# Cross attention: row maxima over pieces of 512 keys with the 65 left over in one, and the values copied by ScalarE with their bias folded through the output matrix

## The chip, the cores and the metric

The kernel runs on one core of a Trainium2 chip (a chip has eight; the others are idle here). The metric is the device time of one execution in microseconds (us); lower is better. One core has five engines that run their own instruction queues in order: TensorE (PE in the rows; PEld is its weight load), VectorE (DVE), ScalarE (ACT), GpSimd (POOL) and SyncE (SP, which here only issues DMAs). They wait for each other through semaphores.

## The reference, cut to what matters

The kernel computes a whole layer: self attention, cross attention on a context of 1601 tokens, a second self attention, a feed-forward block and a mixture of experts. The change lies in the cross attention alone:

```python
# x: (8, 256, 128), ctx_1024: (8, 1601, 128), H = 16 heads of 8
q = split_heads(x @ cq_w + cq_b)
k = split_heads(ctx @ ck_w + ck_b)
v = split_heads(ctx @ cv_w + cv_b)
scores = einsum('bqhd,bkhd->bhqk', q, k) / sqrt(8) + mask
probs = softmax(scores, axis=-1)
ca = einsum('bhqk,bkhd->bqhd', probs, v).reshape(8, 256, 128)
h = ca @ co_w + co_b          # then the residual and a layer norm
```

All is float32. The rows of `probs` sum to one, so a bias on `v` comes out of the attention as the same bias on every row of `ca`, and out of `h` as `cv_b @ co_w`.

## The kernel before, in words

The phases run one after another: self attention (to about 190 us), `phase_cross` (the subject here), self attention, the feed-forward block, the experts. In `phase_cross` a unit of work is a *pair* of heads of one batch: 8 batches x 8 pairs = 64 pairs, numbered g. Four engines work on it at once.

- **Maxima.** For the softmax the greatest score of every query row is found ahead of time, two pairs early. TensorE computes the scores with the queries on the partitions, in pieces that the code calls *grains* (`grain`, L1381, product L1395), and VectorE takes the maximum of each (`maxima`, L1610, L1616). The 1601 keys are cut into four pieces of 401, 401, 401 and 398 (`chunks`, L1301); with 2 heads and 2 tiles of 128 queries that is 16 grains to a pair. Four PSUM banks (`GRAIN`, L1306) hold them: a grain waits until VectorE has read the one four before it (`m_read`, L1387). After the 16th VectorE reduces the pieces to the negated maximum (`negate`, L1619, L1623), GpSimd splits it into three bf16 parts (`split_maxima`, L1708), TensorE turns it (`max_rows`, "m", L1439) and ScalarE writes it as three more rows of the queries (`place_maxima`, L1538).
- **Scores.** TensorE computes them again with the keys on the partitions (`scores`, "s", L1398, product L1413), 13 tiles to a pair of 2 x 256 columns; ScalarE takes the exponential of each (`exponentials`, L1529, L1535).
- **Values.** TensorE multiplies the exponentials with the values and a column of ones (`values`, "v", L1419, product L1433) in three *bursts* (`V_BURSTS`, L1225): tiles 0 to 3, 4 to 7 and 8 to 12. A burst waits for the exponentials of its tiles. Then ScalarE copies the result out (`read_sums`, "o", L1547, L1552).
- **Keys and values of the next batch.** In pairs 0 and 1 of a batch the next context is turned ("T", `turn_context`, L1456, taken by ScalarE, L1557), in pairs 2 and 3 its keys are made ("K", L1465, L1564), in pairs 4 and 5 its values ("V", `make_values`, L1473, product L1477). Each of T, K, V has four rounds per batch, two to a pair. The values are taken from PSUM by VectorE (`take_values`, L1649): one addition of the bias `cv_b` for each tile of 128 tokens (L1656), so four to a round and one in the last, 13 to a batch, into `VP`, where every head's 8 values are followed by a one.

The two heads of a pair lie on different rows of TensorE's array (partitions 0 to 53 and 64 to 117), so a product of one head can run beside a product of the other.

The order of the work is a list written out by `cross_plan` (L1228), which every engine walks through. In step j of 13 it puts a score tile "s" (three tiles ahead of the bursts, so tiles 0 to 2 of the next pair come in steps 10 to 12), a round of T, K or V in steps 5 and 10, the burst in steps 3, 7 and 12 (with "m" ahead of the second), and grains spread evenly: two in step 0, then one, with two in steps 3, 7 and 11, none in step 12. So 4 grains lie ahead of the first burst, 5 between the first and the second, 7 between the second and the third. Three more PSUM banks (`RING`) go round over "s", "m", "c", "e", T, K and V: each waits for the reader of the third before it (`take_bank`, L1362); "m" waits for a round of V in step 5 in this way. The last score tile of a pair is made in two halves ("h"). `grain_order` (L1254) gives each grain to the head that the last score tile did not use.

For the first batch the rounds run before the steps begin (L1521, L1696). SyncE loads the keys of a pair as soon as the scores of the pair a batch earlier are done (`load_keys`, L1791). `co_b` is added at the end of the phase by GpSimd (L1762).

Of the kernel before, what the change touches and what calls it, by code (L numbers as in the profile page):

```python
# [1222 lines left out]


V_BURSTS = (range(0, 4), range(4, 8), range(8, NTILES))  # L1225
# [26 lines left out]


def grain_order(chunks):  # L1254
# [12 lines left out]
def cross_steps(actions):  # L1267

    for step in range(-2, B * PAIRS + 1):
        b, p = divmod(step, PAIRS)  # L1270
        for what, i, ahead in cross_plan(p):
# [5 lines left out]
            elif what in "rc":  # L1277
                if 0 < b < B:
                    actions[what](b - 1, i)
            elif what == "e":  # L1280
                if b == B:
                    actions[what](b - 1, i)
            elif 0 <= step + ahead < B * PAIRS:
                actions[what](step + ahead, i)


def cross_ring():

    turns = [(what, 0, i) for what in "TKV" for i in range(4)]
    cross_steps({what: lambda unit, i, what=what: turns.append((what, unit, i)) for what in "smceTKV"})  # L1290
    return turns


def phase_cross(k):

    nc = k.nc
    T, N, G = NTILES, NCTX, 16
# [4 lines left out]
    grains = grain_order(chunks)  # L1302
    NV = len(V_BURSTS)
# [13 lines left out]
    with ExitStack() as st:  # L1317
# [13 lines left out]
        CT = k.sb("CT", [128, T * 128], stack=st)  # L1331
        KPARTS = k.sb("KPARTS", [128, 3, N], BF16, stack=st)
        KF0 = OT[:, 0:4, :].rearrange("p (c j) n -> p c (j n)", c=2)
        QF = k.CAT[:, :].rearrange("p (c n) -> p c n", c=4)
# [13 lines left out]
        k_made, k_taken, k_split, k_stored = sem("k_made"), sem("k_taken"), sem("k_split"), sem("k_stored")  # L1348
        v_made, v_taken = sem("v_made"), sem("v_taken")
        k_first, q_made, q_taken, q_stored = sem("k_first"), sem("q_made"), sem("q_taken"), sem("q_stored")  # L1350
        q_split = [sem("q_split_first"), sem("q_split_rest")]
# [8 lines left out]
        def _(pe):  # L1360

            def take_bank(what, unit, i):  # L1362

                n = turn[what, unit, i]
                if n >= 3:
# [5 lines left out]
                    elif old in "ce":  # L1371
                        pe.wait_ge(sums_done, a + 1)
                    elif old == "T":
                        pe.wait_ge(ctx_t_taken, 4 * a + j + 1)
# [6 lines left out]
            def grain(g, u):  # L1381
                n = G * g + u
                b, p = batch_of(g)
                s, qt, _, a, w = grains[u]
                half = slice(HALF * s, HALF * s + CROSS_ROWS)
                if n >= NG:
# [93 lines left out]

            prepare = {"T": turn_context, "K": make_keys, "V": make_values}
            def project_self(g):
# [38 lines left out]
            for i in range(4):  # L1521
                make_values(0, i)
            cross_steps({"s": scores, "h": last_tile, "g": grain, "v": values, "m": max_rows, "c": batch_values,
                         "e": last_values, "T": turn_context, "K": make_keys, "V": make_values})

        @block.scalar
        def _(act):
# [39 lines left out]
            def take_first_keys(i):  # L1567
# [7 lines left out]
                last.then_inc(k_taken, 1)  # L1575

            def take_normed(g):
                act.wait_ge(y_turned, g + 1)
# [19 lines left out]
            for g in range(2, 4):  # L1598
                take_normed(g)
                take_queries(g)  # L1600
            act.wait_ge(q_stored, 32 * 4)
            act.wait_ge(k_first, 6)
            act.wait_ge(k_rest, 6)
            cross_steps({"s": exponentials, "m": place_maxima, "o": read_sums, "T": take_turned, "K": take_keys})

        @block.vector
        def _(v):
            nc.vector.memset(k.PO[:, :], 0.0).then_inc(psum_cleared, 1)

            def maxima(g, u):  # L1610
                n = G * g + u
                s, qt, chunk, a, w = grains[u]
# [3 lines left out]
                nc.vector.tensor_reduce(MG[:, g % 4, 2 * s + qt, chunk:chunk + 1], GRAIN[n % NG][:, 0:w],  # L1616
                                        AX.X, ALU.max).then_inc(m_read, 1)

# [29 lines left out]

            def take_values(b, i):  # L1649
                bank = bank_of("V", b, i)  # L1650
                v.wait_ge(v_made, 4 * b + i + 1)
                if i == 0 and b >= 2:
                    v.wait_ge(pv_done, NV * PAIRS * (b - 1))
# [39 lines left out]
            normalise(3)  # L1693
            v.wait_ge(vp_set, 2)
            v.wait_ge(late_in, 48)
            for i in range(4):  # L1696
                take_values(0, i)
            cross_steps({"g": maxima, "neg": negate, "r": reciprocals, "c": scale, "e": divide_last, "V": take_values})

        @block.gpsimd  # L1700
        def _(pl):
# [891 lines left out]
```

## Time and profile before

| | us |
|---|---|
| three runs | 1243.72, 1246.9, 1254.9 (median 1246.9) |
| the profiled execution | 1246.21 |
| its span, first to last instruction | 1244.4 |
| the cross attention's steps (first maxima to last burst) | 221 to about 855 |
| busy in the whole span: PE, DVE, ACT, POOL | 1062.8, 986.2, 855.6, 407.2 |

Busy times overlap, and a product's recorded duration holds its way through the array, so that several matmuls in a row are recorded as lying over each other; the distance between starts is what one costs. The same holds, to a smaller part, for VectorE and ScalarE: a row "x7" with its whole duration is seven instructions back to back. "idle before <-X" is the time in which the engine waited ahead of the group, and who ended the wait.

### The profile page before, as it was taken

What the parts mean: (1) busy time and instruction counts of PE and PEld (TensorE: products, weight loads), DVE (VectorE), ACT (ScalarE), POOL (GpSimd) and SP (SyncE); (2) the same over time, 40 slices, a digit from 0 to 9 for tenths busy, and PEclk for the clock granted to TensorE, in tenths of its full rate; (3) what the DMA queues carried; (4) which work ended last, traced back from release to release, by engine and by line L of the source; (5) the groups of instructions that cost most, each with busy time, mean ns of one, the idle gap of its engine ahead of it and who ended that gap; (6) DMA issues with size and microseconds to landing.
All of it is one profiled execution on the core that took longest, in us unless ns stands there. A gap on an engine that the chain in (4) does not pass through costs nothing. (4 is left out here: it accounts for less than half of the span.)

```text
span 1244.4 us, 32719 instructions
## 1 busy us (share of the span) xinstructions
PE 1062.8 (85%) x11548; PEld 580.2 (47%) x11548; DVE 986.2 (79%) x2786; ACT 855.6 (69%) x1759; POOL 407.2 (33%) x838
## 2 busy tenths in 40 slices
PE   5899966899999999999999999996778879349993
PEld 2455534344444444444444444443334446338883
DVE  7688846789889898898988989992689968766664
ACT  3599944387878878788788887883379855325553
POOL 4222214050140511404105041012533425736662
PEclk8799987699999999999999999998779989669997
DMA  6943036405232143321432204100462031201113
GB/s 190 213 96 68 24 85 153 123 28 129 70 76 67 33 123 76 74 69 33 120 79 64 79 7 117 30 2 7 121 135 70 15 114 51 85 13 46 48 46 119
DMA packets 90178, 96.35 MB, mean 77 GB/s; under 512 B 18569, under 2 KB 76337, under 8 KB 90018
## 3 DMA queue, kind: packets, MB, share of 16 engines
q1 hardware_dynamic: 85922, 87.96, 28.1%
q0 software_dynamic: 2496, 5.12, 1.5%
q8 instruction: 95, 1.56, 0.5%
q10 hardware_dynamic: 1600, 1.18, 0.3%
q14 instruction: 65, 0.53, 0.2%
HBM read 67.62 MB, written 27.82 MB: 77 GB/s over the span
## 5 line engine op out<-in xcount | busy, mean ns | idle before, releaser
L1616 DVE TENSOR_REDUCE MG<-bank 128x1 f32<-128x401 f32 (+1 forms) x1024 | 515.5, 566 | 69.3 <-PE bank L1395 67.7
L1535 ACT ACTIVATE PT<-bank 128x512 f32<-128x512 f32 (+1 forms) x624 | 334.1, 598 | 53.0 <-PE bank L1413 52.7
L1413 PE MATMUL bank<-QP,KP 54*128 54x256 bf16 (+1 forms) x1664 | 253.0, 273 | 10.9 <-ACT PT L1535 1.4
L1395 PE MATMUL bank<-KP,QP 54*128 54x401 bf16 (+1 forms) x1024 | 236.0, 343 | 9.8 <-DMA KP<-ctx_k_parts 4.6
L1433 PE MATMUL bank<-PT,VP 128*9 128x256 f32 (+1 forms) x2688 | 198.0, 367 | 0.8 <-ACT XT L1535 0.8
L1706 POOL TENSOR_TENSOR MP<-MN,ZERO 128x4 bf16<-128x4 f32 x128 | 26.4, 206 | 417.6 <-DVE MN L1623 412.6
L1413 PEld LDWEIGHTS bank<-QP,KP 54*128 54x128 bf16 (+1 forms) x1664 | 111.6, 96 | 100.6 <-ACT PT L1535 24.1
L1395 PEld LDWEIGHTS bank<-KP,QP 54*128 54x128 bf16 x1024 | 75.5, 93 | 119.6 <-DVE MG L1616 98.1
L1535 ACT ACTIVATE XT<-bank 128x512 f32<-128x512 f32 (+1 forms) x208 | 117.1, 599 | 19.9 <-PE bank L1413 19.5
L1040 PE MATMUL bank<-QP,KP 51*128 51x256 bf16 x512 | 91.2, 280 | 16.4 <-DVE MN L1152 7.9
L1433 PEld LDWEIGHTS bank<-PT,VP 128*9 128x9 f32 (+1 forms) x2688 | 76.3, 90 | 58.2 <-issue 21.3
L997 PE MATMUL bank<-KP,QP 51*128 51x256 bf16 x512 | 91.6, 285 | 5.0 <-DVE MG L1146 1.6
L1146 DVE CUSTOM_DVE_ANT_0 JUNK<-bank,UQ 128x256 bf16<-128x256 f32 x256 | 91.9, 421 | 0.0
L1433 PE MATMUL bank<-XT,VP 128*9 128x256 f32 (+1 forms) x896 | 91.3, 367 | 0.0
L1152 DVE TENSOR_REDUCE MN<-bank 128x2 f32<-128x512 f32 x128 | 81.0, 682 | 3.3 <-POOL MP L1214 1.2
L1106 ACT ACTIVATE XT<-bank 128x512 f32<-128x512 f32 x128 | 73.2, 605 | 11.5 <-PE bank L1040 11.1
L1197 POOL TENSOR_TENSOR MP<-MN,ZERO 128x8 bf16<-128x8 f32 x128 | 26.4, 206 | 150.0 <-DVE MN L1159 88.6
L1040 PEld LDWEIGHTS bank<-QP,KP 51*128 51x128 bf16 x512 | 35.2, 95 | 79.1 <-issue 34.1
L959 ACT COPY QP<-bank 3x512 bf16<-3x512 bf16 x96 | 55.1, 574 | 18.1 <-PE bank L1076 16.8
L2278 PE MATMUL bank<-WUP,XP 128*128 x234 | 64.1, 409 | 2.7 <-DVE XP L2447 2.7
L1706 POOL TENSOR_TENSOR KPARTS<-XT,ZERO 128x401 bf16<-128x401 f32 (+1 forms) x56 | 47.6, 851 | 40.4 <-ACT XT L1564 38.2
L1543 ACT COPY QP<-bank 3x256 bf16<-3x256 bf16 x128 | 45.3, 354 | 19.7 <-PE bank L1444 19.0
(287 smaller groups left out, 1855.9 us busy)
## 6 DMA issues: line engine op xcount, KB each, us to landing
KP<-ctx_k_parts SPq DMA_DIRECT2D x128, 100.1 KB
ctx_k_parts<-KPARTS SPq DMA_DIRECT2D x16, 600.4 KB
KP<-ctx_k_parts SPq DMA_DIRECT2D x128, 50.0 KB
CN<-in_ctx SPq DMA_DIRECT2D x8, 768.0 KB
RAW<-in_w_gate_up SPq DMA_DIRECT2D x8, 512.0 KB, 3.8
QP<-q_parts SPq DMA_DIRECT2D x20, 192.0 KB
ctx_k_parts<-KPARTS SPq DMA_DIRECT2D x16, 200.1 KB
UQ<-bias_table SPq DMA_DIRECT2D x4, 768.0 KB, 7.2
```

The lines of the kernel that those rows point to most:

```text
L997: last = nc.tensor.matmul(bank[:, S * qt:S * (qt + 1)], k.QP[rows, p, a:a + 128], k.KP[rows, p, b * S:(b + 1) * S], start=True, stop=True)
L1040: last = nc.tensor.matmul(bank[:, S * t:S * (t + 1)], k.KP[half(s), p, a:a + 128], k.QP[half(s), p, b * S:(b + 1) * S], start=not bias, st ...
L1106: nc.scalar.activation(PT[n % 8], SCORE[n % 3][:, :], ACT.Exp).then_inc(exp_done, 1)
L1146: last = nc.vector.tensor_tensor_reduce(out=JUNK[:, 2 * (n % 2) + q, :], in0=bank[:, S * q:S * (q + 1)], in1=k.UQ[:, 2 * p + s, 128 * q:12 ...
L1152: nc.vector.tensor_reduce(MN[:, u % 3, j, s, :], bank[:, :].rearrange("p (q n) -> p q n", q=QT), AX.X, ALU.max, negate=True).then_inc(grai ...
L1395: nc.tensor.matmul(GRAIN[n % NG][:, 0:w], k.QP[half, p, b * S + 128 * qt:b * S + 128 * (qt + 1)], k.KP[half, p, a:a + w], start=True, stop ...
L1413: return nc.tensor.matmul(bank[0:rows[t], S * at:S * (at + 1)], k.KP[half, p, 128 * t:128 * t + rows[t]], k.QP[half, p, b * S:(b + 1) * S] ...
L1433: last = nc.tensor.matmul(k.PO[32 * c:32 * c + HD + 1, q:q + w], VP[b % 2][0:rows[t], t, 2 * p + s, :], PT[(T * g + n) % NP][0:rows[t], S ...
L1535: nc.scalar.activation(PT[n % NP][0:rows[t], :], bank_of("s", g, t)[0:rows[t], :], ACT.Exp).then_inc(exp_done, 1)
L1616: nc.vector.tensor_reduce(MG[:, g % 4, 2 * s + qt, chunk:chunk + 1], GRAIN[n % NG][:, 0:w], AX.X, ALU.max).then_inc(m_read, 1)
L1706: return nc.gpsimd.tensor_tensor(out, x, ZERO[:, :].broadcast_to(list(x.shape)), ALU.add)
L2278: last = nc.tensor.matmul(bank[j % 2], XP[:, j % 2, a, :], WUP[:, bass.ds(e, 1), b, n0:n0 + FF].rearrange("p a n -> p (a n)"), start=(n == ...
```

## The change

Three things change.

- **Pieces of 512.** A grain is now one of three pieces of 512 keys, or the 65 keys that are left: for each head one grain takes the 65 of both query tiles in two products of 65 columns side by side in one bank, and VectorE reduces them with one instruction of 2 x 65. A pair has 12 wide grains and 2 narrow ones, 14 instead of 16. In the plan two grains lie in step 0, one in each of steps 1 to 10, two in step 11: 4 ahead of the first burst, 4 between the first and the second, 6 between the second and the third, of which the last two are the narrow ones.
- **Values.** ScalarE copies each round (up to 128 x 512) in one instruction; VectorE's 13 additions of a batch go. In the first batch ScalarE does it ahead of its wait for the queries.
- **Bias.** Once, in the pairs 4 and 5 of the first batch, `cv_b` is turned ("R"), copied by ScalarE, multiplied with the output matrix ("W") and added to `co_b` by VectorE.

```diff
-    T, G, LEAD = NTILES, 16, 3
+    T, G, LEAD = NTILES, GRAINS, 3          # GRAINS = 4 * (NCTX // 512) + 2 = 14
...
+        if j == 3 and p in (4, 5):
+            plan.append(("RW"[p - 4], 0, 0))
...
-    rest = [[(s, qt, u, a, w) for qt in range(QT) for u, (a, w) in enumerate(chunks)] for s in range(2)]
+    rest = [[(s, qt, u) for qt in range(QT) for u in range(NCTX // WIDE)] + [(s, None, None)] for s in range(2)]
...
-                nc.tensor.matmul(GRAIN[n % NG][:, 0:w], k.QP[half, p, b * S + 128 * qt:b * S + 128 * (qt + 1)],
-                                 k.KP[half, p, a:a + w], start=True, stop=True).then_inc(m_ready, 1)
+                s, qt, chunk = grains[u]
+                if qt is not None:
+                    grain_product(g, s, qt, GRAIN[n % NG][:, :], WIDE * chunk).then_inc(m_ready, 1)
+                    return
+                for qt in range(QT):
+                    last = grain_product(g, s, qt, GRAIN[n % NG][:, REST * qt:REST * (qt + 1)], EDGE)
+                last.then_inc(m_ready, 1)
...
+            def turn_row(b, i):
+                pe.wait_ge(late_in, 48)
+                nc.tensor.transpose(take_bank("R", b, i)[:, 0:128], k.ROWS[:, ROW["cv_b"], :],
+                                    k.ID[:, :]).then_inc(row_turned, 1)
+            def project_row(b, i):
+                pe.wait_ge(row_read, 1)
+                nc.tensor.matmul(take_bank("W", b, i)[:, 0:128], BV[:, :], k.WVO[:, WQ["C"] + 1, :],
+                                 start=True, stop=True).then_inc(row_made, 1)
...
+            def take_values(b, i):                        # now on ScalarE
+                bank = bank_of("V", b, i)
+                act.wait_ge(v_made, 4 * b + i + 1)
+                if i == 0 and b >= 2:
+                    act.wait_ge(pv_done, NV * PAIRS * (b - 1))
+                m, n = rows[fours[i][-1]], len(fours[i])
+                nc.scalar.copy(VP[b % 2][0:m, 4 * i:4 * i + n, :, 0:HD],
+                               bank[0:m, 0:128 * n].rearrange("p (t h d) -> p t h d", t=n, h=H)).then_inc(v_taken, 1)
...
+                if qt is not None:
+                    out, x = MG[:, g % 4, 2 * s + qt, chunk:chunk + 1], GRAIN[n % NG][:, :]
+                else:
+                    out = MG[:, g % 4, 2 * s:2 * s + 2, N // WIDE]
+                    x = GRAIN[n % NG][:, 0:QT * REST].rearrange("p (q n) -> p q n", q=QT)
+                nc.vector.tensor_reduce(out, x, AX.X, ALU.max).then_inc(m_read, 1)
...
-            def take_values(b, i):                        # was on VectorE
-                for j, t in enumerate(fours[i]):
-                    m = rows[t]
-                    last = nc.vector.tensor_tensor(VP[b % 2][0:m, t, :, 0:HD],
-                                                   bank[0:m, 128 * j:128 * (j + 1)].rearrange("p (h d) -> p h d", h=H),
-                                                   k.ROWS[0:m, ROW["cv_b"], :].rearrange("p (h d) -> p h d", h=H),
-                                                   ALU.add)
-                last.then_inc(v_taken, 1)
+            def add_row(b, i):
+                v.wait_ge(row_made, 1)
+                row = k.ROWS[:, ROW["co_b"], :]
+                nc.vector.tensor_tensor(row, bank_of("W", b, i)[:, 0:128], row, ALU.add).then_inc(row_added, 1)
...
-            pl.wait_ge(late_in, 48)
+            pl.wait_ge(row_added, 1)
```

## Rows read from the trace of the kernel before

**Rows 1.** Windows: stretch, us, busy of PE, PEld, DVE, ACT, POOL, PEclk, DMA, GB/s

```profile
377.00:454.00 77.00, 72.89 (x870) 35.08 (x869) 67.92 (x151) 63.84 (x135) 20.34 (x47) 1.00 0.27 70
```

**Rows 2.** Costliest groups of the page: maxima (L1616, L1152), weight loads of grains (L1395)

```profile
L1616 DVE TENSOR_REDUCE MG<-bank 128x1 f32<-128x401 f32 (+1 forms) x1024 | 515.5, 566 | 69.3 <-PE bank L1395 67.7
...
L1395 PEld LDWEIGHTS bank<-KP,QP 54*128 54x128 bf16 x1024 | 75.5, 93 | 119.6 <-DVE MG L1616 98.1
...
L1152 DVE TENSOR_REDUCE MN<-bank 128x2 f32<-128x512 f32 x128 | 81.0, 682 | 3.3 <-POOL MP L1214 1.2
```

**Rows 3.** Timeline of VectorE, a pair with the reciprocals, last batch

```profile
794.14 0.17 DVE L1623 TENSOR_REDUCE MN<-MG 128x4 f32<-128x16 f32 x1
...
795.51 0.35 DVE L1632 RECIPROCAL SUMS<-SUMS 128x32 f32<-128x32 f32 x1
...
802.92 0.17 DVE L1623 TENSOR_REDUCE MN<-MG 128x4 f32<-128x16 f32 x1
```

**Rows 4.** Timeline of TensorE, a plain pair: start, duration, products

```profile
386.92 0.38 PE L1433 MATMUL bank<-XT,VP 128*9 128x256 f32 x1
387.23 0.34 PE L1395 MATMUL bank<-KP,QP 54*128 54x401 bf16 x2
387.41 0.27 PE L1413 MATMUL bank<-QP,KP 54*128 54x256 bf16 x1
...
389.07 0.40 PE L1433 MATMUL bank<-PT,VP 128*9 128x256 f32 x2
...
389.51 0.69 PE L1433 MATMUL bank<-PT,VP 128*9 128x256 f32 x8
...
392.43 0.81 PE L1433 MATMUL bank<-PT,VP 128*9 128x256 f32 x9
```

**Rows 5.** Timeline of TensorE, the pair before the last, which has no grains

```profile
840.12 0.61 PE L1433 MATMUL bank<-PT,VP 128*9 128x256 f32 x8
...
842.34 0.40 PE L1433 MATMUL bank<-PT,VP 128*9 128x256 f32 x2
...
842.43 1.03 PE L1433 MATMUL bank<-PT,VP 128*9 128x256 f32 x14
...
845.27 0.62 PE L1433 MATMUL bank<-XT,VP 128*9 128x256 f32 x8
```

**Rows 6.** Timeline of ScalarE, copies of the result, around that pair

```profile
838.42 0.37 ACT L1552 COPY OT<-bank 128x256 f32<-128x256 f32 x1 [0.51 <-PE bank L1433]
...
846.61 0.37 ACT L1552 COPY OT<-bank 128x256 f32<-128x256 f32 x1 [0.26 <-PE bank L1433]
```

**Rows 7.** Timeline of VectorE, a plain pair, the maxima after the second burst

```profile
390.51 3.46 DVE L1616 TENSOR_REDUCE MG<-bank 128x1 f32<-128x401 f32 x7 [0.41 <-PE bank L1395]
```

**Rows 8.** Timeline of TensorE, a pair with a round of V, the turning "m"

```profile
371.25 0.23 PE L1444 MATMUL bank<-IDB,MP 128*3 128x128 bf16 x2 [0.57 <-DVE VP L1656]
```

**Rows 9.** Timeline of VectorE, the same pair, the additions of that round

```profile
370.22 0.89 DVE L1656 TENSOR_TENSOR VP<-bank,LATE 128x128 f32<-128x128 f32 x4
```

**Rows 10.** Timeline of ScalarE, the same pair, exponentials around that round

```profile
370.71 1.08 ACT L1535 ACTIVATE PT<-bank 128x512 f32<-128x512 f32 x2 [0.67 <-PE bank L1413]
```

**Rows 11.** Groups of ScalarE by form, a copy into the values of self attention

```profile
L453 ACT COPY VPS<-bank 128x512 f32<-128x512 f32 x4 | 2.3, 585 | 5.5 <-PE bank L394 5.5
```

**Rows 12.** Timeline of TensorE, pair with two rounds of V, second to third burst

```profile
360.65 1.03 PE L1433 MATMUL bank<-PT,VP 128*9 128x256 f32 x14
...
362.86 1.16 PE L1477 MATMUL bank<-WVO,CT 128*128 128x128 f32 x8
...
364.78 0.62 PE L1433 MATMUL bank<-PT,VP 128*9 128x256 f32 x8
```

**Rows 13.** Timeline of TensorE, pair with two rounds of T, second to third burst

```profile
398.77 0.69 PE L1433 MATMUL bank<-XT,VP 128*9 128x256 f32 x8
...
400.64 0.66 PE L1462 MATMUL bank<-ID,CN 128*128 128x128 f32 x4
...
402.06 1.27 PE L1433 MATMUL bank<-PT,VP 128*9 128x256 f32 x24
```

More of the change, by code:

```diff
@@ L1222, in _ @@
             front.sync(sp, qk_in, (take_sums, spread_sums, give_reciprocals, place_reciprocals))
+WIDE = 512
+GRAINS = 4 * (NCTX // WIDE) + 2
 V_BURSTS = (range(0, 4), range(4, 8), range(8, NTILES))
 def cross_plan(p):
-    T, G, LEAD = NTILES, 16, 3
+    T, G, LEAD = NTILES, GRAINS, 3
     what, i = ("T", "T", "K", "K", "V", "V", None, None)[p], 2 * (p % 2)
@@ L1251, in cross_plan, with grain_order @@
     return plan + [("o", 0, 0), ("neg", 0, 2), ("split", 0, 2)]
-def grain_order(chunks):
-    rest = [[(s, qt, u, a, w) for qt in range(QT) for u, (a, w) in enumerate(chunks)] for s in range(2)]
+def grain_order():
+    rest = [[(s, qt, u) for qt in range(QT) for u in range(NCTX // WIDE)] + [(s, None, None)] for s in range(2)]
     order, half = [], 0
@@ L1282, in cross_steps @@
                     actions[what](b - 1, i)
+            elif what in "RW":
+                if b == 0:
+                    actions[what](0, i)
             elif 0 <= step + ahead < B * PAIRS:
@@ L1289, in cross_ring @@
     turns = [(what, 0, i) for what in "TKV" for i in range(4)]
-    cross_steps({what: lambda unit, i, what=what: turns.append((what, unit, i)) for what in "smceTKV"})
+    cross_steps({what: lambda unit, i, what=what: turns.append((what, unit, i)) for what in "smceTKVRW"})
     return turns
@@ L1296, in phase_cross @@
     nc = k.nc
-    T, N, G = NTILES, NCTX, 16
+    T, N, G = NTILES, NCTX, GRAINS
     rows = [min(128, N - 128 * t) for t in range(T)]
@@ L1301, in phase_cross @@
     chunks = [(c * CW, min(CW, N - c * CW)) for c in range(4)]
-    grains = grain_order(chunks)
+    grains = grain_order()
+    EDGE = WIDE * (N // WIDE)
+    REST = N - EDGE
     NV = len(V_BURSTS)
@@ L1332, in phase_cross @@
         KPARTS = k.sb("KPARTS", [128, 3, N], BF16, stack=st)
+        BV = k.sb("BV", [128, 128], stack=st)
         KF0 = OT[:, 0:4, :].rearrange("p (c j) n -> p c (j n)", c=2)
@@ L1349, in phase_cross @@
         v_made, v_taken = sem("v_made"), sem("v_taken")
+        row_turned, row_read, row_made, row_added = (sem(n) for n in ("row_turned", "row_read", "row_made", "row_added"))
         k_first, q_made, q_taken, q_stored = sem("k_first"), sem("q_made"), sem("q_taken"), sem("q_stored")
@@ L1372, in take_bank @@
                         pe.wait_ge(sums_done, a + 1)
+                    elif old == "R":
+                        pe.wait_ge(row_read, 1)
+                    elif old == "W":
+                        pe.wait_ge(row_added, 1)
                     elif old == "T":
@@ L1383, in grain @@
                 b, p = batch_of(g)
-                s, qt, _, a, w = grains[u]
-                half = slice(HALF * s, HALF * s + CROSS_ROWS)
                 if n >= NG:
@@ L1394, in grain, with grain_product @@
                     pe.wait_ge(kp_in[p], LOADS * (b + 1))
-                nc.tensor.matmul(GRAIN[n % NG][:, 0:w], k.QP[half, p, b * S + 128 * qt:b * S + 128 * (qt + 1)],
-                                 k.KP[half, p, a:a + w], start=True, stop=True).then_inc(m_ready, 1)
+                s, qt, chunk = grains[u]
[5 more added lines that the diff above has]
+                last.then_inc(m_ready, 1)
+            def grain_product(g, s, qt, out, a):
+                b, p = batch_of(g)
+                half = slice(HALF * s, HALF * s + CROSS_ROWS)
+                return nc.tensor.matmul(out, k.QP[half, p, b * S + 128 * qt:b * S + 128 * (qt + 1)],
+                                        k.KP[half, p, a:a + out.shape[1]], start=True, stop=True)
             def scores(g, i):
@@ L1479, in make_values @@
                 last.then_inc(v_made, 1)
[L1481 removed]
+            def turn_row(b, i):
[3 more added lines that the diff above has]
+            def project_row(b, i):
+                pe.wait_ge(row_read, 1)
+                nc.tensor.matmul(take_bank("W", b, i)[:, 0:128], BV[:, :], k.WVO[:, WQ["C"] + 1, :],
+                                 start=True, stop=True).then_inc(row_made, 1)
             def project_self(g):
@@ L1523, in _ @@
             cross_steps({"s": scores, "h": last_tile, "g": grain, "v": values, "m": max_rows, "c": batch_values,
-                         "e": last_values, "T": turn_context, "K": make_keys, "V": make_values})
+                         "e": last_values, "T": turn_context, "K": make_keys, "V": make_values, "R": turn_row,
+                         "W": project_row})
         @block.scalar
@@ L1575, in take_first_keys, with read_row @@
                 last.then_inc(k_taken, 1)
+            def take_values(b, i):
[6 more added lines that the diff above has]
+                               bank[0:m, 0:128 * n].rearrange("p (t h d) -> p t h d", t=n, h=H)).then_inc(v_taken, 1)
+            def read_row(b, i):
+                act.wait_ge(row_turned, 1)
+                nc.scalar.copy(BV[:, :], bank_of("R", b, i)[:, 0:128]).then_inc(row_read, 1)
             def take_normed(g):
@@ L1600, in _ @@
                 take_queries(g)
+            act.wait_ge(vp_set, 2)
+            for i in range(4):
+                take_values(0, i)
             act.wait_ge(q_stored, 32 * 4)
@@ L1603, in _ @@
             act.wait_ge(k_rest, 6)
-            cross_steps({"s": exponentials, "m": place_maxima, "o": read_sums, "T": take_turned, "K": take_keys})
+            cross_steps({"s": exponentials, "m": place_maxima, "o": read_sums, "T": take_turned, "K": take_keys,
+                         "V": take_values, "R": read_row})
         @block.vector
@@ L1611, in maxima @@
                 n = G * g + u
-                s, qt, chunk, a, w = grains[u]
                 if u == 0 and g >= 4:
@@ L1615, in maxima @@
                 v.wait_ge(m_ready, n + 1)
-                nc.vector.tensor_reduce(MG[:, g % 4, 2 * s + qt, chunk:chunk + 1], GRAIN[n % NG][:, 0:w],
-                                        AX.X, ALU.max).then_inc(m_read, 1)
+                s, qt, chunk = grains[u]
+                if qt is not None:
[4 more added lines that the diff above has]
+                nc.vector.tensor_reduce(out, x, AX.X, ALU.max).then_inc(m_read, 1)
             def negate(g, i):
@@ L1693, in _ @@
             normalise(3)
-            v.wait_ge(vp_set, 2)
             v.wait_ge(late_in, 48)
-            for i in range(4):
-                take_values(0, i)
-            cross_steps({"g": maxima, "neg": negate, "r": reciprocals, "c": scale, "e": divide_last, "V": take_values})
+            cross_steps({"g": maxima, "neg": negate, "r": reciprocals, "c": scale, "e": divide_last, "W": add_row})
         @block.gpsimd
```

4 lines of the change are left out of this document (removed).

## The prediction

> **What bounds the kernel now.** I read the page first, then the windows over the cross attention, then the timelines of single pairs, engine by engine. In a stretch of about eight pairs three engines look full: of 77 us PE is busy for 72.9, DVE for 67.9, ACT for 63.8, at a granted clock of 1.00, which is 2.4 GHz [rows 1]. By these shares VectorE, whose maxima fill most of it and whose idle time is 67.7 us of waiting for grains over the whole phase [rows 2], could be the bound. The timelines say it mostly isn't.
>
> The pair with the reciprocals shows it. From one negated maximum to the next it takes 802.92 - 794.14 = 8.78 us, with an addition and a reciprocal (0.35 us and more) put into VectorE's queue [rows 3]; a plain pair also takes 8.78 to 8.79 (20 of the 64 pairs are plain, that is without rounds of T, K or V, and have grains). Half a microsecond more of VectorE cost nothing. So I cut a plain pair at TensorE's bursts:
> - A, from the third burst of the last pair to the first burst, and that burst;
> - B, end of the first to the second: from 386.92 + 0.38 = 387.30 to 389.07, 1.78 [rows 4];
> - the second burst;
> - C, end of the second to the third: from 389.51 + 0.69 = 390.20 to 392.43, 2.23 [rows 4];
> - the third burst. A and the three bursts are the other 4.77.
>
> The last pair but one has no grains, for no pair is left to be prepared. There B is 842.34 - 840.73 = 1.61 and C is 845.27 - 843.46 = 1.81 [rows 5]; the whole is 846.61 - 838.42 = 8.19 [rows 6], which is 0.59 less, so A and the bursts stay. That is what grains cost the chain of a plain pair: 0.17 in B and 0.42 in C, 0.59 of 8.78. Everything else is the loop between exponentials and products (bank free, scores, exponential, burst).
>
> Where the 0.59 lies can be seen. After a burst the first grain goes ahead of the next score tile and uses the same rows of the array: grain at 387.23, tile at 387.41, 0.18 later [rows 4], about 401 columns at 2.4 GHz (0.167). That happens in B and in C: 2 x 0.17. The other 0.25 of C is VectorE: it takes up its seven grains 0.30 after the burst, at 390.51 [rows 7]; the last of them can be issued only when the third is read, at 390.51 + 2 x 0.482 + 0.566 = 392.04, then comes one score tile and the burst at 392.43. The pitch of 0.482 is (3.46 - 0.566) / 6 [rows 2, 7].
>
> **The parts, one by one.**
>
> *Wide pieces, duration.* Self attention has a reduction of 512 elements: 0.682, against 0.566 for 401 [rows 2], so 0.116 for 111 elements, 1.045 ns each. A wide grain's pitch is then 0.482 + 0.116 = 0.598 and a narrow one's (130 elements) 0.199. VectorE's maxima of a pair go from 16 x 0.482 = 7.71 to 12 x 0.598 + 2 x 0.199 = 7.57: 0.14 a pair, which matters only in C.
>
> *Wide pieces, the grain ahead of the score tile.* 512 columns take 0.213, so +0.046 in B and +0.046 in C. Bounds: 0, if the tile's rows are free earlier, and +0.10 for each.
>
> *C of a plain pair.* The chain over VectorE becomes: burst end + 0.30 + 0.046, then the last narrow grain waits for the second wide one instead of the third: 0.598 + 0.682 = 1.28 instead of 1.53. It is issued at about +1.69 instead of +1.90. The exponentials' own chain, 1.81 + 0.213, would allow the burst at +2.03. So C becomes about 2.03 to 2.10 instead of 2.23; I take -0.20. Bounds: -0.25 (all of VectorE's wait) and 0 (the four small products with four weight loads take up what the wait gives). With +0.05 in B a plain pair gains 0.15, and 20 of them 3.0 us.
>
> *Pairs with T, K or V, 42 of them.* There C isn't set by VectorE. With a turned round of 0.66 in step 10 C is 402.06 - 399.46 = 2.60 [rows 13]; with a round of V of 1.16 it is 364.78 - 361.68 = 3.10 [rows 12]: longer by exactly the difference of the two rounds on TensorE, although VectorE has four additions in the second as well. So nothing is gained there from VectorE, and the longer grains cost +0.05 in B and, as a second wide grain lies ahead of the tile after the round while the narrow ones then save a part, +0.06 in C. 42 x 0.11 = 4.6 us lost. Bounds: -0.05 a pair (the narrow grains save more than the wide ones cost), -2.1, and +0.20, +8.4.
>
> *Values on ScalarE.* In B of the pairs 4 and 5 the "m" product needs the bank of V. The round ends and VectorE starts its four additions at 370.22, done 0.89 later at 371.11 [rows 9]; "m" has stood idle for 0.57 and goes at 371.25 [rows 8]. ScalarE was idle for 0.67 up to 370.71 [rows 10], so it can take the copy at 370.22 too. The same copy exists, into the values of self attention, with the same shape and stride: 0.585 [rows 11]. "m" then goes at about 370.22 + 0.585 + 0.09 (the lag after 371.11 was 0.14) = 370.9 to 371.0, after 0.3 less; against the later burst I count -0.23 for each of 14 pairs, 3.2 us gained. Behind the copy in ScalarE's queue stands the next exponential, which today starts at 370.71 because its scores come then; the copy (pitch about 0.49, see the third rival) frees the engine at the same moment. In C the copy of pair 4 falls into a gap of the same kind, and C is TensorE's there. Bounds: -0.35 a pair, and 0.
>
> *VectorE's 13 additions a batch* were covered by this (in B they end the wait of "m", counted above; in C nobody waits for them). The four rounds of the first batch lie beside a wait for keys. If this cover were wrong, they would be worth up to 7 x 13/4 x 0.89 = 20.2 us, see the first rival.
>
> *First two steps.* They have no scores yet, VectorE is the bound: -0.14 each, -0.3. *The bias*, once: a turn, a product, two ring places, an addition: +0.6, between 0 and 1.5; of these instructions none repeats.
>
> The Trainium skill speaks against moving the values: "ScalarE: Activation LUTs", Rules for kernel authors, has additions and the like on VectorE, not ScalarE. The trace goes against it here: four additions take 0.89, one copy of all four 0.585 [rows 9, 11], since the bias no longer has to be added. By the rule B would not get shorter, and the sum would be 3.2 us higher.
>
> The skill's "TensorE: Matmul & The Clock Gate", What overlaps and what doesn't, says that a weight load overlaps running matmuls only on other rows of the array. The row shows 0.18 between two products on the same rows with 0.167 of columns [rows 4], so next to nothing of the load is exposed behind a wide piece. Whether a piece of 65 columns hides it no row shows; by the rule it doesn't, which is the second rival's mechanism.
>
> **Sum.** 1246.2 (profiled execution; span 1244.4 and 1.8 around it) - 3.0 - 3.2 - 0.3 + 4.6 + 0.6 = 1244.9. The median of the runs lies 0.7 above the profiled execution, so 1245.6 us, no change that can be told (about 1% is what can be told here; the three runs alone lie 0.9% apart).
>
> **Rivals.**
> - *VectorE is the bound after all.* For it: 67.9 of 77 us busy, and TensorE often stands before a grain. Against: the reciprocals' pair, and A unchanged by the absence of grains, B by no more than a grain's columns. Then every microsecond off VectorE counts: 64 x 0.14 = 9.0 and 20.2 for the additions, so 1246.2 - 29.2 = 1217.0. Chance 0.10.
> - *The narrow pieces cost TensorE more than they save* (the side of slower). Four products of 65 columns (0.027 each) with four weight loads of about 0.093 [rows 2] stand between the last score tiles of C. If the loads aren't hidden, and neither half runs beside the other, they put 4 x 0.12 = 0.48 behind the tile's 0.21, where 0.32 is now: +0.37 for the 42 pairs, while the plain ones keep only their wait. 42 x (0.11 + 0.37) = 20.2 and 20 x 0.07 = 1.4, less 3.5 and plus 0.6: 1264.9. It decides from about 0.3 a pair. Against: 0.18 for a grain and its load. Chance 0.07.
> - *ScalarE's copies push the exponentials back.* Four to a batch at a pitch of 1.08 - 0.59 = 0.49 [rows 10, 11], 7 x 4 x 0.49 = 13.7 at most, and the gain of 3.2 gone: 1244.9 + 3.2 + 13.7 = 1261.8. It decides if ScalarE has less than 0.49 of idle time at the copy; it has 0.67 in the row. Chance 0.03.
>
> **How the numbers follow.** Forecast 0.80, rivals 0.10, 0.07, 0.03. The forecast's own ends: all terms low, 1246.9 - 5.0 - 2.1 - 4.9 - 0.3 = 1234.6; all high, 1246.9 - 0.3 + 8.4 + 1.5 = 1256.5, which needs every bound at once; I end at 1254. So 1234 to 1254, which leaves out the rivals, 0.2. Faster by over 1% 0.11, within 1% 0.79, slower by over 1% 0.10.
>
> **What would show it.** Plain pairs of about 8.63 (8.78 now); B in plain pairs 1.83; C 2.03 to 2.1; pairs 4 and 5 with B shorter by some 0.2 and no wait of "m" for the values; pairs with T and K longer by 0.05 to 0.15; wide maxima at 0.68, narrow at about 0.28; copies into VP of 0.585. VectorE's busy time drops by some 25 us while the span doesn't. If plain pairs fall below 8.4, or pairs with T or K get shorter, VectorE set more than I allow; if the distance between the last tiles of C grows by 0.3, the narrow pieces are dear. Either would make the prediction wrong.

## The result, and the profile after

The changed kernel takes 1234.05 us in the median of 4 runs (1231.04 to 1235.04), the one before 1248.33 (1243.72 to 1254.9, 4 runs). The ratio is 0.9885, with a 95% interval of 0.9856 to 0.9915: faster by 1.15%. I had forecast 1245.6 and no change that can be told; the gain is more than that. That the time still lies inside my range, by 0.05 us, is luck: the pairs with T, K or V gained well beyond the low end of their term, and other terms and the scatter of the runs made up for it. The profiled execution took 1234.46 (1246.21 before) and its span 1232.6 (1244.4).

The groups of maxima on the page after, and the forms of VectorE's groups (the columns are those of [rows 2]), then the windows over the same 77 us as [rows 1]:

```profile
L1672 DVE TENSOR_REDUCE MG<-bank 128x1 f32<-128x512 f32 (+1 forms) x896 | 503.4, 626 | 95.5 <-PE bank L1419 93.7
...
L1419 PEld LDWEIGHTS bank<-KP,QP 54*128 54x128 bf16 x1024 | 75.1, 95 | 109.2 <-DVE MG L1672 63.4
```

```profile
L1672 DVE TENSOR_REDUCE MG<-bank 128x1 f32<-128x512 f32 x768 | 477.7, 683 | 95.5 <-PE bank L1419 93.7
...
L1672 DVE TENSOR_REDUCE MG<-bank 128x2 f32<-128x130 f32 x128 | 31.0, 285 | 0.0
```

```profile
377.00:454.00 77.00, 73.72 (x889) 35.80 (x885) 65.56 (x125) 66.46 (x141) 20.63 (x48) 1.00 0.28 72
```

The durations are the forecast ones: 0.683 for 512 elements, 0.285 for 2 x 65. VectorE has less to do (65.6 of 77 us, 67.9 before) and waits more (95.5 us, 69.3 before); the clock of TensorE is 1.00 in both. The page agrees (VectorE busy for 955.0 us of the whole span, 986.2 before). So the whole-phase view says only that VectorE was relieved. Where the time went shows when the pairs are cut at TensorE's bursts, as in the prediction. A plain pair after, TensorE and VectorE:

```profile
452.65 0.61 PE L1457 MATMUL bank<-PT,VP 128*9 128x256 f32 x8
453.20 0.40 PE L1419 MATMUL bank<-KP,QP 54*128 54x512 bf16 x2
453.43 0.39 PE L1437 MATMUL bank<-QP,KP 54*128 54x256 bf16 x4
...
455.09 0.40 PE L1457 MATMUL bank<-PT,VP 128*9 128x256 f32 x2
...
455.18 1.03 PE L1457 MATMUL bank<-PT,VP 128*9 128x256 f32 x14
...
457.45 0.23 PE L1419 MATMUL bank<-KP,QP 54*128 54x65 bf16 x2
...
458.25 0.62 PE L1457 MATMUL bank<-XT,VP 128*9 128x256 f32 x8
```

```profile
456.57 2.89 DVE L1672 TENSOR_REDUCE MG<-bank 128x1 f32<-128x512 f32 x6 [0.35 <-PE bank L1419]
459.50 0.17 DVE L1678 TENSOR_REDUCE MN<-MG 128x4 f32<-128x16 f32 x1
```

B is 455.09 - 453.26 = 1.83 (1.78 before [rows 4]), C is 458.25 - 456.21 = 2.04 (2.23), and VectorE's maxima after the second burst take 2.89 for six instead of 3.46 for seven [rows 7]. That is the forecast of 1.83 and 2.03 to 2.1. The same cut through all pairs, in us, each the median over the batches 1 to 6:

("First" and "second" are the two pairs of a batch with rounds of the same kind.)

| kind of pair | B before, after | C before, after |
|---|---|---|
| plain | 1.78, 1.82 | 2.23, 2.03 |
| first, second with T | 2.26, 2.30 / 2.28, 2.30 | 2.60, 2.51 / 2.46, 2.51 |
| with K (both) | 2.33, 2.31 | 2.88, 2.69 |
| first, second with V | 2.84, 2.42 / 2.84, 2.42 | 3.10, 2.91 / 2.46, 2.51 |

A is 1.33 and the bursts 1.05, 1.12 and 1.27 in both kernels; only in the pair with the head sums ("c", the first with K) A went from 1.93 to 2.02. Summed from the first copy of the result to the last (607.4 us before, 596.3 after):

| | before | after | difference | forecast |
|---|---|---|---|---|
| 20 plain pairs | 176.3 | 173.2 | -3.0 | -3.0 |
| 13 with T | 125.1 | 125.4 | +0.3 | |
| 14 with K | 143.5 | 141.1 | -2.4 | |
| 14 with V, without the one-off steps | 145.8 | 138.8 | -7.1 | |
| T, K and V together | | | -9.2 | +4.6 - 3.2 = +1.4 |
| one-off steps for the bias (A 1.82 and 1.98 in two pairs) | | 1.1 | +1.1 | +0.6 |

The two steps without scores, from the first maximum to the second negated one, went from 15.73 to 15.49, close to the forecast 0.3. Pairs and first steps together are 11.4 of the 11.75 between the two profiled executions. The medians lie 14.3 apart; the other 2.5 is where these two executions stand in the scatter of their kernels' runs. The rounds' pairs are where the forecast failed.

Behind the round of K in C, after:

```profile
428.33 0.94 PE L1494 MATMUL bank<-CT,WQK 128*128 128x398 f32 x2
429.20 0.39 PE L1419 MATMUL bank<-KP,QP 54*128 54x512 bf16 x3
429.43 0.40 PE L1437 MATMUL bank<-QP,KP 54*128 54x256 bf16 x4
429.64 0.22 PE L1419 MATMUL bank<-KP,QP 54*128 54x65 bf16 x2
429.80 0.38 PE L1457 MATMUL bank<-XT,VP 128*9 128x256 f32 x1
```

The same place before:

```profile
430.44 0.94 PE L1470 MATMUL bank<-CT,WQK 128*128 128x398 f32 x2
431.31 0.34 PE L1395 MATMUL bank<-KP,QP 54*128 54x401 bf16 x1
431.49 0.40 PE L1413 MATMUL bank<-QP,KP 54*128 54x256 bf16 x4
431.70 0.50 PE L1395 MATMUL bank<-KP,QP 54*128 54x401 bf16 x2
432.13 0.38 PE L1433 MATMUL bank<-XT,VP 128*9 128x256 f32 x1
```

From the end of the round to the burst it was 432.13 - 431.38 = 0.75 and is 429.80 - 429.27 = 0.53. And in B of a V pair, TensorE, then ScalarE:

```profile
433.93 1.16 PE L1501 MATMUL bank<-WVO,CT 128*128 128x128 f32 x8
...
435.85 0.22 PE L1468 MATMUL bank<-IDB,MP 128*3 128x128 bf16 x2 [0.22 <-ACT VP L1617]
```

```profile
435.12 0.59 ACT L1617 COPY VP<-bank 128x512 f32<-128x512 f32 x1
435.66 0.60 ACT L1569 ACTIVATE PT<-bank 128x512 f32<-128x512 f32 x1
```

"m" stood idle for 0.22 instead of 0.57 [rows 8]. The round began 0.48 after the first burst's end (433.45); the same pair before had begun its round 0.60 after.

### The profile page after: what moved, and what is told of

It reads as the page before. It is cut to its first block and busy times, and to the rows that moved or that the text cites. A ratio compares the mean times of both kernels' runs of the same rounds, so it can differ in the third digit from the quotient of the medians.

```text
span 1232.6 us, 32530 instructions
## 1 busy us (share of the span) xinstructions
PE 1050.8 (85%) x11551; PEld 576.2 (47%) x11551; DVE 955.0 (77%) x2555; ACT 869.3 (71%) x1792; POOL 405.9 (33%) x838
## 5 line engine op out<-in xcount | busy, mean ns | idle before, releaser
L1672 DVE TENSOR_REDUCE MG<-bank 128x1 f32<-128x512 f32 (+1 forms) x896 | 503.4, 626 | 95.5 <-PE bank L1419 93.7
L1437 PE MATMUL bank<-QP,KP 54*128 54x256 bf16 (+1 forms) x1664 | 267.1, 274 | 15.0 <-ACT PT L1569 5.1
L1419 PE MATMUL bank<-KP,QP 54*128 54x512 bf16 (+1 forms) x1024 | 217.0, 343 | 8.8 <-DMA KP<-ctx_k_parts 5.0
L1437 PEld LDWEIGHTS bank<-QP,KP 54*128 54x128 bf16 (+1 forms) x1664 | 108.4, 95 | 117.4 <-ACT PT L1569 39.5
L1152 DVE TENSOR_REDUCE MN<-bank 128x2 f32<-128x512 f32 x128 | 80.9, 683 | 3.5 <-POOL MP L1214 1.2
```

What stands on the lines that cost most here:

```text
L1152: nc.vector.tensor_reduce(MN[:, u % 3, j, s, :], bank[:, :].rearrange("p (q n) -> p q n", q=QT), AX.X, ALU.max, negate=True).then_inc(grai ...
L1419: return nc.tensor.matmul(out, k.QP[half, p, b * S + 128 * qt:b * S + 128 * (qt + 1)], k.KP[half, p, a:a + out.shape[1]], start=True, stop ...
L1437: return nc.tensor.matmul(bank[0:rows[t], S * at:S * (at + 1)], k.KP[half, p, 128 * t:128 * t + rows[t]], k.QP[half, p, b * S:(b + 1) * S] ...
L1672: nc.vector.tensor_reduce(out, x, AX.X, ALU.max).then_inc(m_read, 1)
```

## The experiments

**The two halves alone.** First the pieces without the rest.

```diff
-        if j == 3 and p in (4, 5):
-            plan.append(("RW"[p - 4], 0, 0))
...
+            def take_values(b, i):                        # on VectorE again, with the bias, as before
```

> The pieces of 512 alone: the values stay with VectorE and their 13 additions, and the one-off steps for the bias are gone. Chain theory (a pair's time is the loop of score tiles, exponentials and bursts; only TensorE's own grains and the bank that 'm' waits for lie on it): plain pairs 8.63 us as after the change, pairs with K and the stretch C of the first V pair as after (2.69, 2.91), stretch B of V pairs longer by the difference of four additions and one copy, 0.89 - 0.59 = 0.30, so 2.72 instead of 2.42. From first to last copy of the result 596.3 + 14 x 0.30 - 1.1 (the one-off steps) = 599.4 us, total some 3 us above the changed kernel, 9 below the one before. Rival (VectorE is the bound): the additions put back cost up to 20 us, total some 1250.

Median 1239.86 us, ratio to the kernel before 0.9915 (0.9887 to 0.9943). Plain pairs 8.63, K pairs with C 2.69, first V pair C 2.91, B of the V pairs 2.72, each to the hundredth what was expected; from first to last copy 597.8 (the last burst alone is 1.05 shorter in this execution than in the one of the changed kernel, 1.27 against 2.31; without that 598.9).

Then the copies and the folded bias on the kernel before:

```diff
-                for j, t in enumerate(fours[i]):
-                    last = nc.vector.tensor_tensor(VP[b % 2][0:m, t, :, 0:HD], ...
+                nc.scalar.copy(VP[b % 2][0:m, 4 * i:4 * i + n, :, 0:HD],
+                               bank[0:m, 0:128 * n].rearrange("p (t h d) -> p t h d", t=n, h=H)).then_inc(v_taken, 1)
```

> The other half alone: values copied by ScalarE and their bias through the output matrix, on the kernel before with its 16 pieces of 401. Chain theory: plain pairs stay at 8.78, T and K pairs as before, stretch B of V pairs 2.84 - 0.30 = 2.54; first to last copy of the result 607.4 - 4.2 + 1.1 = 604.3 us, total 3 us below the kernel before (1245). Rival (VectorE is the bound): 20 us less.

Median 1245.53 us, ratio 0.9953 (0.9924 to 0.9982). B of the V pairs 2.54, everything else as in the kernel before; 603.0 us (604.0 with the same last burst). So the halves add: B of V pairs loses 0.12 by the pieces and 0.30 by the copy, 0.42 together. The copies are worth 14 x 0.30 less 1.1 for the one-off steps, the pieces 8.5 us, and 2.5 of that lie in K pairs and 2.9 in V pairs, for which I had forecast a loss from the pieces. In the copies' run the stretches C of the V pairs (3.10 and 2.46) are those of the kernel before, so ScalarE's copies delay nothing there.

**What makes the pieces pay behind a round.** The same instructions, the narrow pieces first:

```diff
-    rest = [[(s, qt, u) for qt in range(QT) for u in range(NCTX // WIDE)] + [(s, None, None)] for s in range(2)]
+    rest = [[(s, None, None)] + [(s, qt, u) for qt in range(QT) for u in range(NCTX // WIDE)] for s in range(2)]
```

> The changed kernel with the two pieces of 65 keys of a head taken first in a pair instead of last; the same instructions in another order. Theory of the narrow pieces (behind the round in step 10 TensorE is the bound, and what stands between the round and the third burst counts in full, so narrow pieces there save 0.2 us): stretch C of K pairs goes from 2.69 back to about 2.90, of the first V pair from 2.91 to 3.1; in plain pairs C goes from 2.03 to 2.1 to 2.25, since the last piece is wide. First to last copy 596.3 + 21 x 0.2 + 20 x 0.1 = 602.5 us. Rival (the gain of K pairs comes from VectorE having less to do, or from fewer pieces at all): no change from the order, 596.3.

C of the K pairs is 2.84, of the first V pair 3.07, of the first T pair 2.56: 0.15, 0.16 and 0.05 of what had been gained are gone. So most of the gain is the place of the narrow pieces, between the last round and the third burst. What remains, 2.88 - 2.84 = 0.04, no run isolates; the columns behind the round, below, account for it. In plain pairs C stayed at 2.02, where I had expected 2.1 to 2.25: the last piece is on the other head's rows than the last tile, so its width doesn't delay the tile. The pair with the head sums has A at 1.87 now, 0.15 less, since its first pieces are narrow; so the total is 597.0 (598.0 with the long last burst) and not 602.5. TensorE in C of the K pair:

```profile
430.95 0.94 PE L1494 MATMUL bank<-CT,WQK 128*128 128x398 f32 x2
431.82 0.40 PE L1419 MATMUL bank<-KP,QP 54*128 54x512 bf16 x2
432.05 0.39 PE L1437 MATMUL bank<-QP,KP 54*128 54x256 bf16 x4
432.26 0.38 PE L1419 MATMUL bank<-KP,QP 54*128 54x512 bf16 x1
432.57 0.38 PE L1457 MATMUL bank<-XT,VP 128*9 128x256 f32 x1
```

Round to burst is 432.57 - 431.89 = 0.68, against 0.53 with the narrow pieces last and 0.75 before. `grain_order` says why. Of the three grains behind the round, before, all three are of the second head: 401 + 401 + 398 columns on its rows of the array. In the changed kernel the second head has one wide and one narrow grain there, 512 + 130 columns, and the third grain runs beside them on the other head's rows; in this run it has two wide ones, 1024. At 2.4 GHz the differences are 558 columns or 0.23, and 382 columns or 0.16; the rows show 0.22 and 0.15. So what counts behind the round is the columns on the rows of the head that has most to do. The 0.07 between this run and the kernel before (0.75 to 0.68) is of the same kind (176 columns, 0.07); the round itself begins 0.04 later, behind a longer wide piece, which leaves the 0.04 above.

**Is it VectorE's time or the bank?** The additions given back to VectorE, on a spare tile:

```diff
+            def refill(b, i):
+                v.wait_ge(v_made, 4 * b + i + 1)
+                for j, t in enumerate(fours[i]):
+                    nc.vector.tensor_tensor(SPARE[:, j, :], k.ROWS[:, ROW["cv_b"], :], k.ROWS[:, ROW["fo_b"], :], ALU.add)
```

> The changed kernel, with four additions of 128 x 128 (one in the last round) given back to VectorE in each round of V, on a spare tile that nobody waits for; the output is the same. Chain theory: 0 us, at most 1 (first to last copy 596.3 to 597.3 us). Rival (VectorE's work counts): up to 7 x 13 x 0.22 = 20 us more.

Nothing: plain, K and V pairs are the same to 0.05 us in their sums, first to last copy 596.4 (597.4 with the long last burst; 1.1 more than the changed kernel's, all of it in the second pairs with T, where in single batches the reciprocals wait for their DMA, by amounts that vary from run to run). VectorE has the four additions in its queue again and "m" waits for ScalarE's copy as before:

```profile
433.81 3.68 DVE L1673 TENSOR_REDUCE MG<-bank 128x1 f32<-128x512 f32 x6 [0.61 <-PE bank L1420]
437.41 0.89 DVE L1713 TENSOR_TENSOR SPARE<-LATE 128x128 f32<-128x128 f32 x4
438.21 3.30 DVE L1673 TENSOR_REDUCE MG<-bank 128x1 f32<-128x512 f32 x5
```

And the copy itself given to VectorE, one instruction a round:

```diff
-                nc.scalar.copy(VP[b % 2][0:m, 4 * i:4 * i + n, :, 0:HD],
+                nc.vector.tensor_copy(VP[b % 2][0:m, 4 * i:4 * i + n, :, 0:HD],
```

> The changed kernel with the values' one copy a round given to VectorE instead of ScalarE (the bias stays folded). Theory (what counts is how soon the bank of the round is free, not whose time it takes): a VectorE instruction of 512 elements takes 0.68 (its reduction), ScalarE's copy 0.59, so stretch B of V pairs goes from 2.42 to about 2.52; first to last copy of the result 596.3 + 14 x 0.1 = 597.7 us. Rival (the gain is VectorE's relief): as without the relief, B 2.72 or more, 600.5.

VectorE's copy takes 0.688, B of the V pairs is 2.53 (2.42 + 0.10), 1.5 us more in the V pairs, first to last copy 597.5:

```profile
L1698 DVE COPY VP<-bank 128x512 f32<-128x512 f32 x24 | 16.5, 688 | 7.6 <-PE bank L1501 7.5
```

So of the 0.30 the one instruction for four, which the folded bias allows, gives 0.19, and that it runs on ScalarE 0.11. The relief of VectorE gives nothing, as the additions given back show.

**The chain put to use.** If a wide piece ahead of the score tile costs its columns, it should stand behind the tile:

```diff
+        plan += held
+        held = []
...
-        plan += [("g", g, 2) for g in range(G * (j + 1) // T if j else 0, min(G, G * (j + 2) // T))]
+        fresh = [("g", g, 2) for g in range(G * (j + 1) // T if j else 0, min(G, G * (j + 2) // T))]
+        if j in (3,):
+            held = fresh
+        else:
+            plan += fresh
```

> The changed kernel with one move in the plan: the grain of step 3, which stands right behind the first burst, goes behind the next score tile. Chain theory (a wide grain ahead of the tile costs its columns, 0.21 us, in the chain of exponentials): stretch B of plain pairs from 1.82 to the 1.61 of a pair without grains; in pairs with a round B is bound by TensorE's work up to the round, so 0 to -0.05 there; first to last copy of the result 596.3 - 20 x 0.21 = 592.1 us. Rival (VectorE needs that grain in time): B unchanged or longer, as VectorE, which is left without a grain for 0.2 us more, holds up the next ones.

B of plain pairs 1.61, as in a pair without grains; the first T pair 2.09 (-0.21) and K pairs 2.21 (-0.10) gained too, where I had expected next to nothing; V pairs 2.42, unchanged. 589.9 us, time 1229.44 (one run). The last burst was the short one in this execution and in all that follow, so 1.0 of a distance to the changed kernel's 596.3 is not the move's.

ScalarE's queue shows the reason in T and K pairs. In the changed kernel it runs an exponential, a second one, the copy of the round and the next exponential without a pause, starting at 471.10, 471.60, 472.07 and 472.54 in a first T pair: there the bound is ScalarE from the first tile's scores on, not TensorE's work up to the round. With the tile first this row begins 0.21 earlier after the burst and stays without a pause in the T pair, so B is shorter by all of 0.21. In a K pair the copy has to wait for the longer round (exponentials from 491.83, copy at 492.93 instead of some 0.1 earlier), and B is shorter by 0.10 only.

With `j in (3, 7)`:

> The same, and the grain of step 7 behind the first tile after the second burst as well. Theory (in a plain pair the chain through VectorE's first two maxima bounds stretch C: burst end + 0.35 + 1.28 + the rest): the first of them starts some 0.25 to 0.4 later, so C of plain pairs goes from 2.03 to 2.2 to 2.3, and what B gained is lost again; first to last copy 592.1 + 20 x 0.2 = 596 us. Rival (in C too only the grain ahead of the tile counts): C goes to 1.81, first to last copy 588 us or less.

Theory and rival were each partly right. C of plain pairs went to 2.16, so VectorE's chain does take over there:

```profile
449.18 0.23 PE L1425 MATMUL bank<-KP,QP 54*128 54x65 bf16 x2
449.78 0.20 PE L1425 MATMUL bank<-KP,QP 54*128 54x65 bf16 x1 [0.36 <-DVE MG L1678]
```

```profile
448.43 2.89 DVE L1678 TENSOR_REDUCE MG<-bank 128x1 f32<-128x512 f32 x6 [0.26 <-PE bank L1425]
```

The second narrow piece waits for the second maximum (448.43 + 0.60 + 0.68 = 449.71). But C of all pairs with rounds fell by 0.2 (T 2.29, K 2.49, V 2.72 and 2.31): again I had the plain pairs right and the others wrong. 582.2 us, time 1220.06 (one run).

Then the narrow piece of one head right behind the second burst, without the other moves:

```diff
+    rest[early].insert(heads[:8].count(early), rest[early].pop())     # early: the head whose turn the ninth grain is
```

> The changed kernel with the piece of 65 keys of one head moved from the last place to the place right behind the second burst (the same instructions). Chain theory: in stretch C what stands ahead of the tile is then 0.05 instead of 0.21, and the last piece of a pair waits for a narrow and a wide one instead of two wide ones: C of plain pairs from 2.03 to about 1.87, C of the pairs bound by the exponential (second T, second V) from 2.51 to 2.35, and of K and the first V pair nearly as now (2.69 and 2.91: -0.15 in front, +0.08 at the end). First to last copy 596.3 - 20 x 0.16 - 20 x 0.16 - 21 x 0.05 = 589 us. Rival (the narrow pieces count by their number at the end of the pair only): plain pairs unchanged, K pairs longer by 0.08, 598 us.

Plain C 1.87, second T and second V 2.36 and 2.35, first T 2.41, K and first V unchanged at 2.69 and 2.91; 589.2 us, time 1229.89 (one run). That is as expected for plain and second pairs. For K I had -0.15 in front and +0.08 at the end; they came out equal, since the piece moved is the second head's, which leaves 1024 columns on its rows behind the round: round to burst is 0.68 again. With the move of step 3, and with the one-off steps ahead of the pairs:

```diff
-    turns = [(what, 0, i) for what in "TKV" for i in range(4)]
+    turns = [(what, 0, i) for what in "TKV" for i in range(4)] + [("R", 0, 0), ("W", 0, 0)]
```

> The tile ahead of the grain after the first burst, the narrow piece behind the second burst, and the one-off steps for the bias ahead of the pairs, where TensorE waits for keys. Chain theory, adding the three: -4.2, -7.3, -1.1 against the changed kernel, first to last copy 583.7 us, total some 1222 us, faster than both kernels. Rival (the moves take from each other, as VectorE's chain then bounds C): no more than 5 us gained, 591.

583.9 us against 583.7 expected; median 1221.09 us, ratio 0.9777 (0.9754 to 0.9800).

**The best version.** All moves together:

> Both grains behind the tile after their burst, the narrow piece of one head first in stretch C, and the one-off steps for the bias ahead of the pairs. Chain theory: B 1.61 in plain pairs; C of plain pairs, which VectorE's first two maxima held at 2.16 with both moved, back to 1.85 to 1.9 since the first of them is narrow; C of K and the first V pair 2.49 and 2.72, up to 0.08 more as only one narrow piece is left at the end. First to last copy 582.2 - 20 x 0.28 - 1.1 + 1 = 576.5 us, total some 1214, faster than all kernels so far. Rival (VectorE still holds up C): plain C stays at 2.16 and the sum at 581.

Median 1213.01 us (1210.42 to 1217.05), ratio to the kernel before 0.9733 (0.9706 to 0.9761): more than twice the gain of the change, with the same work. 574.8 us from first to last copy (575.9 with the long last burst). B 1.61 and C 1.81 in plain pairs, which is what a pair without grains has [rows 5]: the maxima no longer cost them anything.

```profile
444.27 0.62 PE L1470 MATMUL bank<-PT,VP 128*9 128x256 f32 x8
444.82 0.28 PE L1450 MATMUL bank<-QP,KP 54*128 54x256 bf16 x1
...
446.50 0.40 PE L1470 MATMUL bank<-PT,VP 128*9 128x256 f32 x2
...
446.59 1.03 PE L1470 MATMUL bank<-PT,VP 128*9 128x256 f32 x14
447.55 0.39 PE L1450 MATMUL bank<-QP,KP 54*128 54x256 bf16 x3
447.69 0.47 PE L1432 MATMUL bank<-KP,QP 54*128 54x65 bf16 x3
...
449.43 0.62 PE L1470 MATMUL bank<-XT,VP 128*9 128x256 f32 x8
```

B is 446.50 - 444.89 = 1.61, C 449.43 - 447.62 = 1.81; after each burst the tile now comes first. K and first V pairs have C at 2.49 and 2.72, the same as with both tiles first, without the 0.08 that I had added because only one narrow piece is left at the end. Here it is the first head's piece that moved, so 512 + 130 columns stay on the second head's rows, and round to burst is 0.53: what counts is whose piece is left, not how many.

## Why the prediction was wrong, and where it was right

**Right.** The reading of the loop held: VectorE isn't the bound. The first rival would have asked 20 us for the additions; given back, they cost nothing. So the sign that I had named for it, K pairs getting shorter, came true without VectorE being the cause: the sign was badly chosen. Plain pairs came out at 8.63, as written, with B and C each to 0.01. The second rival (dear weight loads of the narrow pieces) is out: their place is what gains. ScalarE's copies pushed no exponential back: one starts at 435.66, right behind the copy, 0.42 after the first product of its tile (435.24); the same pair before shows 0.42 as well (437.65 and 438.07).

**The step that failed** is "Pairs with T, K or V, 42 of them". It put +0.11 on each, +4.6 us, and bounded it below by -0.05. The pieces alone gave K pairs -2.5 and V pairs -2.9 and left T pairs as they were: -5.5 us, 10 away from the term. For C of the pairs with long rounds I had the bound right, TensorE's own work up to the burst, and then looked at the grain ahead of the tile alone. Two things were left out:
- In C three grains stand between the round and the burst, where TensorE is the bound, and before all three are on one head's rows (1200 columns, now 642). I wrote that they "then save a part" and let the longer wide piece outweigh it. The rows now show 0.75 before and 0.53 after; with the narrow pieces moved to the front 0.68. In K and the first V pair C fell by 0.19, of which the place of the narrow pieces is 0.15. In the second pairs with T and V, whose second round is short, C did rise by the forecast 0.05.
- In B a grain less stands ahead of the round of V (step 3 has one instead of two): B fell by 0.12 from the pieces alone, where I had +0.05. The rounds of T and K begin 0.12 earlier too, but there B ends on ScalarE's row of exponentials: +0.04 and -0.02.

The bound below was taken from nothing that the rows showed: two grains with 0.17 us of columns each were replaced by two with 0.05, so 0.2 a pair was open. With the term at its measured -5.5, and the two terms below at theirs, the forecast would have been 1245.6 - 10.1 - 1.0 + 0.5 = 1235.0; measured were 1234.05.

**Mis-sized terms.** The copy: 14 x 0.23 forecast, 14 x 0.30 measured. The first count was right (four additions 0.89, one copy 0.59); I rounded the gain down for a longer lag that isn't there. The one-off steps: 0.6 forecast, 1.1 measured (A 1.33 to 1.82 and 1.98 in the two pairs, which shows that they stood in the chain of A).

**Where rules and rows differ.** With the copy on ScalarE B became shorter by 0.30, and 0.11 of that is lost on VectorE; the Trainium skill's "ScalarE: Activation LUTs", Rules for kernel authors, puts additions on VectorE, and kept there they cost these 0.30. The rule speaks of additions; here the bias is folded, and what is left is a copy, which it does not name. By the Trainium skill's "TensorE: Matmul & The Clock Gate", What overlaps and what doesn't, a weight load waits for matmuls on its own rows. The trace differs here for the narrow pieces: their two products, on the same rows with a weight load each, start 0.04 apart (457.45, two in 0.23 where one is recorded with 0.19), while a load is recorded with 0.095; the second product's load must lie over the first product.

**Open.** Why K pairs gain 0.10 in B from the tile going first, and the first T pair 0.21, is read from ScalarE's rows and not tested by a run of its own. The reciprocals' wait for their DMA I did not take apart; in the second T pair of single batches it grew to 2.8 us in B (4.88, against 2.09 without a wait) in the faster kernels.

## What to carry to other kernels

Cut the loop at an event that ends each turn and compare turns with and without the suspected work: one pair without grains gave the price of the grains (0.59 us, which the best version then won back to 0.01 us) and the place of each part, which the busy shares (three engines at 83 to 95%) could not. Then do this for every kind of turn, not for the plain one alone; where an engine is the bound between two events, list what a change takes out of its queue there before pricing what it adds, and on TensorE list it by the rows of the array, since products on other rows run beside. And in an in-order queue the place of an instruction is worth as much as its length: four small moves gained some 20 us on top of the change's 14.

## What I had not expected of the hardware

Products of 65 columns with their own weight loads start 0.04 us apart on the same rows (0.027 of columns each), so the load of 0.095 costs next to nothing even behind a short product. Behind a round the time to the burst followed the columns on one head's rows to 0.01 us in three orders (1200, 1024 and 642 columns: 0.75, 0.68, 0.53). VectorE's copy of 128 x 512 from PSUM takes 0.688 us and ScalarE's 0.586. And pairs of one kind repeat to 0.01 us over the batches wherever no DMA wait falls in, so that a change of 0.05 us a pair can be read from a single profile, while whole runs of one kernel lie up to 1% apart.
